# Two head groups in one output bank, three part writes instead of six, and the next x transposed ahead of the maxima

## The chip, the cores and the metric

The kernel runs on one core of one Trainium2 chip. The metric is device time in microseconds from start to end of the whole program. The kernel before took 684.7 us as the median of three runs (683.92 to 686.21).

## What is computed

The input is x, 8 sequences of 512 tokens and 128 features, fp32. It is normalised over its features, and one transformer layer's two halves are added to it side by side:

```python
xn = layernorm(x)
x  = x + attention(xn) + moe(xn)
```

The attention has 16 heads of 8 features, a causal mask, a softmax, and an output projection with a bias. The other half is a mixture of 8 experts (176 hidden columns each, the best 2 per token weighted by a softmax router) and a shared expert of 352 columns; each is `silu(x @ wg) * (x @ wu) @ wd`.

## The kernel before

One sequence of 512 tokens is one block; there are eight. Each engine has its own program, written out by hand in order, and waits on semaphores that count up over the blocks. The steady part is a loop whose pass holds two stages: `attend(i)`, the attention of block i, and `experts_and_maxima(i + 1)`, the expert half of the next block together with the row maxima of its scores. Names and lines below are those of the kernel before.

**Expert stage.** The hidden columns are 14 tiles of 128 (`NT`), in the order `TILE_ORDER`, the three shared ones first. For tile k TensorE computes gate and up (`gate_up`, L457 to L459: an fp32 product out of three reduced ones, six matmuls in all, in the first three of four "ring" banks) and, two tiles later, the down product into `bank_y` (L468 to L470). ScalarE takes the silu (L736) and a rounded copy (L743), GpSimd weighs by the router (L839) and takes the rest of the rounding (L845), VectorE multiplies gate and up (L1066).

**Maxima.** The softmax needs the row maxima ahead. 20 "pairs" of score tiles per block (`scores`, L486, with the mask by L477) are each reduced by VectorE (L1084). `PAIRS_AT[k]` says how many go beside tile k, and `AHEAD = 1` puts pair 0 at the very end of the attention stage before. Pairs 0 to 4 share one pair of banks (the ring's last and `bank_m`), so each waits for the maximum of the one before; from pair `ONE_SLOT` = 5 on, two pairs of banks alternate. Pair 0 waits for `ops_loaded[0]`, pair 10 for `ops_loaded[1]`: the first and second half of the heads' q and k in their split form.

**That split form.** q and k are each written as bf16 parts (`split_q`, `split_k` on VectorE, L981 to L987), sent to DRAM by the SP queue (`q_parts_out`, `k_parts_out`: six DMAs each, three for the heads in the lower half of the partitions and three for the upper), and read back as `q_op` and `k_op` with 6 terms x 8 features = 48 rows a half (`operands_in`, L361 and L363, four DMAs for every half of the heads). SP's order in the loop is: k out, q out, `operands_in` half 0, router weights out and (after they have landed) back in 18 broadcasts (L347), `operands_in` half 1, the store of the output, the maxima out and back (`maxima_in`, L373 and L377).

**End of the expert stage.** When the last pair is reduced, `split_maxima` makes three bf16 parts on VectorE (L1099 to L1106); beside k = 12 TensorE transposes them (`transpose_maxima`, L529), ScalarE copies them out (L753), and SP writes them to DRAM and reads them back as three more rows of `q_op`. VectorE normalises the next block's x (L962) after that split; TensorE transposes it (`transpose_x`, L408) after the maxima, and ScalarE copies it (L710) after the maxima's rows. Then come the next block's k projection and router logits and, when the maxima's rows have landed, the first unit of the attention (L559).

**Attention stage.** It has four groups of four heads, five units a group: TensorE makes transposed scores (`scores_t`, L559), ScalarE the exponentials (L784, 128x1024 each, two such outputs in flight), GpSimd the mask (L872). One group later `weigh_v` (L587) multiplies by v. Every head has 32 output rows, of which 9 are used: 8 features and the row sum from a column of ones in `v_op`. Group g's four heads fill `nat[:, g % 2]`; VectorE copies that bank out (`take_o`, L1113), TensorE transposes it (`transpose_o`, L603) into `o_banks[g]`, VectorE takes reciprocals and multiplies (`normalise_o`, L1119, L1121). So each of these is done four times a block: three of the `transpose_o` stand in the attention stage, one in k = 2 of the next expert stage. The gate and up products of the next block's tiles 0 and 1 stand at the end of the attention stage, between the last parts of `weigh_v`.

Of the kernel before, what the change touches and what calls it, by code (L numbers as in the profile page):

```python
# [13 lines left out]
P = 128  # L14
NB = 8
# [7 lines left out]
GROUPS = H // 4  # L23
NE = 8
# [64 lines left out]
def block_kernel(nc, x, wqkT, wvT, b_qk, b_v, woT, b_o, gateT, w_gu, w_dn, ident, causal, lower, out):  # L89
    ctx = ExitStack()  # L90
    with ctx:
# [41 lines left out]
        v_op = sb("v_op", [P, QT, H, 32])  # L133
# [6 lines left out]
        o_rden = sb("o_rden", [P, QT, 4, 1])  # L140
# [38 lines left out]
        o_banks = [bank_y, bank_m, bank_y, banks[:, 5, :]]  # L179
# [3 lines left out]
        q_dram = nc.dram_tensor("q_dram", [2, TERMS, DH, PAIRS, S], BF16, kind="Internal").ap()  # L183
        k_dram = nc.dram_tensor("k_dram", [2, TERMS, DH, PAIRS, S], BF16, kind="Internal").ap()
# [87 lines left out]
        PART_WRITES = 6  # L272
# [23 lines left out]
        def _(sp):  # L296
            def tokens_in(n):
# [25 lines left out]
            def k_parts_out(j):  # L323
                sp.wait_ge(ksplit_step, 4 * j + 4)
                for s in range(2):
                    own = k_parts[HALF * s:HALF * (s + 1), :, :]
                    for first, n in ((0, 3), (3, 2), (5, 1)):
                        sp.dma_start(k_dram[s, first:first + n].rearrange("t d i n -> (d i) t n"),
                                     own[:, 0:n, :]).then_inc(k_written, 16)

            def q_parts_out(j):
                sp.wait_ge(qsplit_step, 4 * j + 4)
                for s in range(2):
# [15 lines left out]
            def operands_in(j, i, n):  # L349
# [9 lines left out]
                for s in range(2):  # L359
                    rows = slice(HALF * s, HALF * s + SROWS)  # L360
                    sp.dma_start(q_op[rows, own, :], q_dram[s, :, :, own, :].rearrange("t d i n -> (t d) i n")  # L361
                                 ).then_inc(ops_loaded[n], 16)
                    sp.dma_start(k_op[rows, own, :], k_dram[s, :, :, own, :].rearrange("t d i n -> (t d) i n")  # L363
                                 ).then_inc(ops_loaded[n], 16)
# [38 lines left out]
        def _(pe):  # L403
# [57 lines left out]
            def down(b, k, i):  # L461
# [3 lines left out]
                if k == 0 and i is not None:  # L465
                    pe.wait_ge(o_normed, GROUPS * i + 3)
# [22 lines left out]
            def scores(b, i, g, v):  # L489
# [6 lines left out]
                if n == 0:  # L496
                    if i is None:
                        pe.wait_ge(combT_done, 1)
                    else:
                        pe.wait_ge(exp_done, ST_ALL * i + ST_ALL - 1)  # L500
                        pe.wait_ge(o_normed, GROUPS * i + 2)
# [72 lines left out]
            def weigh_v(i, g, c, front):  # L574
# [18 lines left out]
            def transpose_o(i, g, front):  # L593
                pe.wait_ge(o_taken, GROUPS * i + g + 1)
                bank = o_banks[g]
                if g == 0:
                    pe.wait_ge(base_done, i + 1)
                elif g == 1 and front:
                    pe.wait_ge(combT_done, i + 2)
                elif g == 2:  # L600
                    pe.wait_ge(o_normed, GROUPS * i + 1)
                for q in range(QT):
                    mm = pe.transpose(bank[:, q * P:(q + 1) * P], o_sb[:, g % 2, q * P:(q + 1) * P],  # L603
# [3 lines left out]
            def transpose_on(i):  # L607
                pe.wait_ge(o_normed, GROUPS * i + GROUPS)
# [14 lines left out]
            def experts_and_maxima(b, i, front):  # L623

                n = 0 if i is None else AHEAD
                for k in range(NT + 2):
                    if k < NT and (k >= 2 or i is None):
                        gate_up(b, k)
                    if k == 2 and i is not None:
                        transpose_o(i, 3, True)  # L630
                    late = int(k < 4 and PAIRS_AT[k] > 1)
                    for _ in range(PAIRS_AT[k] - late + (AHEAD if k == 0 and i is None else 0)):
# [46 lines left out]
            pe.wait_ge(small_loaded, 13 * 16)  # L679
# [16 lines left out]
            transpose_o(NB - 1, 3, False)  # L696
# [5 lines left out]
        def _(act):  # L702
# [42 lines left out]
            def experts(b, i, front):  # L745
                for k in range(NT):
# [544 lines left out]
```

## Time and profile before

| | |
|---|---|
| profiled execution | 684.85 us, its span 683.1 us |
| median of three runs | 684.7 us |
| TensorE busy | 575.0 us (84%) |
| VectorE / ScalarE / GpSimd busy | 479.9 / 347.6 / 347.7 us |
| mean granted TensorE clock | 0.951 of full |
| moved by DMA | 57.13 MB, 84 GB/s over the span |

The profile is of one execution. Busy time is counted per engine; the span runs from its first instruction to its last. Times in the views are microseconds from the start of the span. One steady block takes 78 to 79 us, and the views below look mostly at one pass, from about 248 us to about 299 us.

### The profile page before, as it was taken

How to read it: one execution, taken by the hardware profiler on the slowest of the kernel's cores; microseconds unless marked ns; L12 is line 12 of the kernel's file. 1: busy time of each engine (PE TensorE's matmuls, PEld its weight loads, DVE VectorE, ACT ScalarE, POOL GpSimd, SP SyncE). 2: the span in 40 equal slices, each digit the busy share in tenths (PEclk: the TensorE clock that was granted, in tenths of full speed). 3: DMA queues.
4: the chain of work that ended last, by engine and by line, in shares of the span. 5: the costliest groups of instructions: out<-in, count | busy, mean ns of one | idle time of the engine just before them, and what ended most of it. 6: DMA issues, size and time to landing. Idle time of an engine off the chain costs nothing.

```text
span 683.1 us, 12744 instructions
## 1 busy us (share of the span) xinstructions
PE 575.0 (84%) x4208; PEld 325.3 (48%) x4208; DVE 479.9 (70%) x829; ACT 347.6 (51%) x472; POOL 347.7 (51%) x330
## 2 busy tenths in 40 slices
PE   1239989799979989899897989899898989799895
PEld 1115652466526653466524653356534654256422
DVE  4947977389656988389665987479774896569713
ACT  1413368233873358533683349533584339543581
POOL 3505735277243854368253764258353773438542
PEclk9759999999999999999999999999999999999987
DMA  6855003830248003750148101660037302480000
GB/s 172 247 123 140 1 22 83 197 64 16 52 93 215 8 13 75 173 107 15 31 102 204 22 21 47 148 161 15 6 92 194 68 15 52 101 209 10 13 2 16
DMA packets 44439, 57.13 MB, mean 84 GB/s; under 512 B 5936, under 2 KB 29840, under 8 KB 44240
## 3 DMA queue, kind: packets, MB, share of 16 engines
q1 hardware_dynamic: 44416, 56.83, 34.4%
q8 instruction: 13, 0.21, 0.1%
q14 instruction: 10, 0.08, 0.0%
HBM read 41.60 MB, written 15.20 MB: 83 GB/s over the span
## 4 chain that ended last, share of the span: by engine, by line
PE 59%; DVE 19%; DMA 9%; issue 6%; SPq 3%; ACT 2%; DVEq 1%; POOLq 0%; POOL 0%; ACTq 0%
PE banks L457 8%; PE banks L459 7%; PE banks L458 7%; PE banks L486 7%; DMA k_op<-k_dram 6%; PE banks L468 5%; PE banks L477 4%; DVE neg_max L1084 4%; PE banks L559 3%; PE banks L587 3%; PE banks L470 3%; PE banks L469 3%; PE banks L603 2%; DVE max_parts L1104 2%; ACT probs L784 1%
## 5 line engine op out<-in xcount | busy, mean ns | idle before, releaser
L1084 DVE TENSOR_REDUCE neg_max<-banks 128x2 f32<-128x1024 f32 (+3 forms) x224 | 194.7, 915 | 71.0 <-PE banks L477 70.1
L784 ACT ACTIVATE probs<-banks 128x1024 f32<-128x1024 f32 x160 | 156.9, 1030 | 19.6 <-PE banks L559 16.5
L839 POOL TENSOR_TENSOR probs<-probs,cb 128x512 f32<-128x512 f32 x88 | 115.9, 1317 | 94.1 <-ACT probs L736 93.2
L845 POOL TENSOR_TENSOR hid_lo<-probs,hid_hi 128x512 fp32r<-128x512 f32 (+1 forms) x88 | 113.4, 1289 | 90.9 <-ACT hid_hi L743 90.9
L736 ACT ACTIVATE probs<-banks 128x512 f32<-128x512 f32 (+1 forms) x112 | 67.0, 598 | 167.9 <-PE banks L459 167.3
L872 POOL TENSOR_SCALAR_AFFINE_SELECT probs<-probs 128x512 f32<-128x512 f32 x128 | 91.9, 739 | 118.9 <-ACT probs L784 118.9
L457 PE MATMUL banks<-x_hi,w_hi 128*128 128x512 f32 (+1 forms) x224 | 96.7, 432 | 2.8 <-DVE w_lo L1230 2.7
L587 PE MATMUL banks<-probs,v_op 128*32 128x512 f32 (+3 forms) x1024 | 95.8, 447 | 0.3
L459 PE MATMUL banks<-x_hi,w_lo 128*128 128x512 f32 (+1 forms) x224 | 92.1, 411 | 0.0
L743 ACT ACTIVATE hid_hi<-probs 128x512 fp32r<-128x512 f32 (+1 forms) x112 | 70.3, 628 | 42.5 <-DVE probs L1066 41.6
L458 PE MATMUL banks<-x_lo,w_hi 128*128 128x512 f32 (+1 forms) x224 | 91.6, 409 | 0.0
L486 PE MATMUL banks<-k_op,q_op 48*128 48x384 bf16 (+3 forms) x512 | 62.0, 304 | 34.5 <-DMA k_op<-k_dram 26.7
L1066 DVE TENSOR_TENSOR probs<-probs,banks 128x512 f32<-128x512 f32 (+1 forms) x112 | 76.0, 680 | 19.8 <-POOL probs L839 10.4
L559 PE MATMUL banks<-q_op,k_op 51*128 51x384 bf16 (+3 forms) x512 | 62.6, 307 | 4.4 <-ACT probs L784 2.3
L468 PE MATMUL banks<-hid_hi,wd_hi 128*128 128x512 f32 (+1 forms) x112 | 56.6, 505 | 2.3 <-DVE hid_lo L1074 2.2
L486 PEld LDWEIGHTS banks<-k_op,q_op 48*128 48x128 bf16 x512 | 19.5, 94 | 75.5 <-issue 34.5
L477 PE MATMUL banks<-mask_half,ident_half 64*128 64x256 bf16 (+1 forms) x640 | 55.3, 250 | 0.0
L559 PEld LDWEIGHTS banks<-q_op,k_op 51*128 51x128 bf16 x512 | 17.6, 94 | 72.9 <-ACT probs L784 42.0
L457 PEld LDWEIGHTS banks<-x_hi,w_hi 128*128 128x128 f32 (+1 forms) x224 | 43.3, 193 | 16.3 <-issue 7.5
L459 PEld LDWEIGHTS banks<-x_hi,w_lo 128*128 128x128 f32 (+1 forms) x224 | 43.8, 196 | 11.2
L458 PEld LDWEIGHTS banks<-x_lo,w_hi 128*128 128x128 f32 (+1 forms) x224 | 44.3, 198 | 8.7
L470 PE MATMUL banks<-hid_lo,wd_hi 128*128 128x512 f32 (+1 forms) x112 | 45.3, 405 | 0.0
(113 smaller groups left out, 634.6 us busy)
## 6 DMA issues: line engine op xcount, KB each, us to landing
cb<-c_dram SPq DMA_DIRECT2D x32, 256.0 KB, 4.3
q_op<-q_dram SPq DMA_DIRECT2D x32, 192.0 KB, 5.6
k_op<-k_dram SPq DMA_DIRECT2D x32, 192.0 KB, 6.2
cb<-c_dram SPq DMA_DIRECT2D x16, 224.0 KB, 4.4
q_dram<-q_parts SPq DMA_DIRECT2D x16, 192.0 KB, 2.7
k_dram<-k_parts SPq DMA_DIRECT2D x16, 192.0 KB, 2.7
cb<-c_dram SPq DMA_DIRECT2D x16, 192.0 KB, 4.5
cb<-c_dram SPq DMA_DIRECT2D x16, 160.0 KB, 4.6
```

Of the source, the lines that this page charges most:

```text
L457: pe.matmul(bank, w_hi[:, w, cols], x_hi[:, :], start=True, stop=False)
L458: pe.matmul(bank, w_hi[:, w, cols], x_lo[:, :], start=False, stop=False)
L459: pe.matmul(bank, w_lo[:, w, cols], x_hi[:, :], start=False, stop=True).then_inc(ready, 1)
L468: pe.matmul(bank_y[:, :], wd_hi[0:n, tile, :], hi, start=(k == 0), stop=False)
L486: pe.matmul(bank[:, a, at:at + n], q_op[own, h // 2, qt * P:n], k_op[own, h // 2, 0:n], start=first, stop=False, skip_group_check=True)
L559: mm = pe.matmul(bank[:, at:at + S - kb * P], k_op[r:r + rows, h // 2, kb * P:(kb + 1) * P], q_op[r:r + rows, h // 2, kb * P:S], start=Tru ...
L587: mm = pe.matmul(nat[32 * j:32 * j + 32, g % 2, kb * P:S], v_op[:, kb, 4 * g + j, :], probs_of(g, j, kb), start=(c == 0), stop=(c == 3), t ...
L784: nc.scalar.activation(probs[:, g % 2, 2 * u:2 * u + 2, :], ring[:, at:at + 2, :], ACT.Exp).then_inc(exp_done, 1)
L839: nc.gpsimd.tensor_tensor(sg[k % 3][:, :], sg[k % 3][:, :], cb[:, TILE_ORDER[k], :], ALU.mult).then_inc(weighted, 1)
L845: nc.gpsimd.tensor_tensor(hid_lo[0:n, k % 3, :], hid[k % 3][0:n, :], hid_hi[0:n, k % 3, :].bitcast(F32), ALU.subtract).then_inc(hid_lo_don ...
L872: return nc.gpsimd.affine_select(out=view, in_=view, compare_op=ALU.is_ge, fill=0.0, base=0, pattern=[[0, 4], [1, P]], channel_multiplier=-1)
L1084: return nc.vector.tensor_reduce(out, in_, AX.X, ALU.max, negate=True)
```

## The change

Three edits.

1. *Output banks.* Groups 0 and 1 accumulate in one bank, groups 2 and 3 in the other. `v_op` gets zeros in the first 9 columns for every odd group, whose own 9 columns come behind them, so that the two groups' sums lie side by side in the 32 rows. `take_o`, `transpose_o` and `normalise_o` then run twice a block, over twice as many columns where they read them. GpSimd places v with four copies instead of one, and `wo_sb` is loaded by four DMAs in the heads' new order instead of one.
2. *Transfers.* The order of the dimensions in the DRAM buffers becomes term, half, feature, pair, token, so each write covers all 128 partitions and there are three a tensor instead of six. The reads keep their number.
3. *Order of work.* Pair 0 moves from the end of the attention stage to k = 1 of the expert stage. The next block's x is normalised on VectorE at tile 0, and transposed and copied before the maxima. The transposed router weights move from (1, 4) to (2, 0) on TensorE, and on VectorE `take_combT` and `split_x` stand before the first `take_o`.

```diff
-AHEAD = 1
-PAIRS_AT = [0 if k < 2 else 2 if k < 11 else int(k == 11) for k in range(NT + 2)]
-ONE_SLOT = AHEAD + 4
+PAIRS_AT = [int(k in (1, 11)) + 2 * int(2 <= k <= 10) for k in range(NT + 2)]
+ONE_SLOT = 5
...
-        v_op = sb("v_op", [P, QT, H, 32])
+        v_op = sb("v_op", [P, QT, 2, H // 2, 32])
...
-        o_banks = [bank_y, bank_m, bank_y, banks[:, 5, :]]
+        o_banks = [bank_y, nat[:, 0, :]]
...
-        q_dram = nc.dram_tensor("q_dram", [2, TERMS, DH, PAIRS, S], BF16, kind="Internal").ap()
+        q_dram = nc.dram_tensor("q_dram", [TERMS, 2, DH, PAIRS, S], BF16, kind="Internal").ap()
...
-                     (wo_sb[:, :], woT), (bo_bc[:, :], b_o.partition_broadcast(P))]
+                     (bo_bc[:, :], b_o.partition_broadcast(P))]
...
+            for j in range(4):
+                sp.dma_start(wo_sb[32 * j:32 * j + 32, :], woT.rearrange("(g j d) e -> j g d e", j=4, d=DH)[j]
+                             ).then_inc(small_loaded, 16)
...
-                for s in range(2):
-                    own = q_parts[HALF * s:HALF * (s + 1), :, :]
-                    for first, n, part in ((0, 3, 0), (3, 2, 1), (5, 1, 2)):
-                        sp.dma_start(q_dram[s, first:first + n].rearrange("t d i n -> (d i) t n"),
-                                     own[:, part:part + 1, :].to_broadcast([HALF, n, S])
-                                     ).then_inc(q_written, 16)
+                for first, n, part in ((0, 3, 0), (3, 2, 1), (5, 1, 2)):
+                    sp.dma_start(q_dram[first:first + n].rearrange("t s d i n -> (s d i) t n"),
+                                 q_parts[:, part:part + 1, :].to_broadcast([P, n, S])).then_inc(q_written, 16)
...
-                    sp.dma_start(q_op[rows, own, :], q_dram[s, :, :, own, :].rearrange("t d i n -> (t d) i n")
-                                 ).then_inc(ops_loaded[n], 16)
+                    sp.dma_start(q_op[rows, own, :], q_dram[:, s, :, own, :]).then_inc(ops_loaded[n], 16)
...
     (weigh_v, TensorE)
-                    if g < 2 and front:
-                        pe.wait_ge((q_done, k_done)[g], i + 2)
-                    if g >= 2:
-                        pe.wait_ge(o_taken, GROUPS * i + g - 1)
+                    if g % 2 == 0 and front:
+                        pe.wait_ge((q_done, k_done)[g // 2], i + 2)
+                bank = nat[:, g // 2, :]
                 for j in range(4):
-                    mm = pe.matmul(nat[32 * j:32 * j + 32, g % 2, kb * P:S], v_op[:, kb, 4 * g + j, :],
-                                   probs_of(g, j, kb), start=(c == 0), stop=(c == 3),
+                    mm = pe.matmul(bank[32 * j:32 * j + 32, kb * P:S], v_op[:, kb, g % 2, 4 * (g // 2) + j, :],
+                                   probs_of(g, j, kb), start=(c == 0 and g % 2 == 0), stop=(c == 3 and g % 2 == 1),
...
     (experts_and_maxima, TensorE, at MAXIMA_AT)
-                        transpose_maxima(b)
                         if front:
                             transpose_x(b + 1)
+                        transpose_maxima(b)
...
     (attend, TensorE)
-                        if u == 2 and g in (2, 3, 4):
-                            transpose_o(i, g - 2, front)
+                        if (g, u) == (3, 2):
+                            transpose_o(i, 0)
                         if front:
-                            if (g, u) == (GROUPS, 1):
-                                pair(i + 1, i, 0)
-                            if (g, u) == (1, 4):
+                            if (g, u) == (2, 0):
                                 transpose_comb(i + 1)
...
     (experts, ScalarE, k == NT - 2)
+                        if front:
+                            take_xT(b + 1)
                         act.wait_ge(mT_ready, b + 1)
...
-                        if front:
-                            take_xT(b + 1)
...
     (experts_and_maxima, VectorE)
+                    if k == 0 and front:
+                        normalise(b + 1)
                     if k == 1 and i is not None:
-                        normalise_o(i, 2)
-                        take_o(i, 3)
+                        take_o(i, 1)
                     if k == 2 and i is not None:
-                        normalise_o(i, 3)
+                        normalise_o(i, 1)
...
     (attend, VectorE, after split_q)
+                    take_combT(i + 1)
+                    split_x(i + 1)
                 take_o(i, 0)
...
```

`k_dram`, `k_parts_out` and the read of `k_op` change as those of q do. The lines in brackets name the place; they are not part of the diff.

## Rows read from the trace of the kernel before

**Rows 1.** The page, busy time by engine: busy us, share of the span, instructions.

```profile
PE 575.0 (84%) x4208; PEld 325.3 (48%) x4208; DVE 479.9 (70%) x829; ACT 347.6 (51%) x472; POOL 347.7 (51%) x330
```

**Rows 2.** The waits of the whole span: total us, times, longest.

```profile
PE banks L486 <- DMA k_op<-k_dram: 26.7, 8, 5.6
```

**Rows 3.** TensorE's timeline, one pass: start, us, line, matmuls, idle before and releaser.

```profile
270.21 0.66 PE L603 MATMUL banks<-ident_sb,o_sb 128*128 128x128 f32 x4 [0.92 <-DVE o_sb L1113]
...
275.43 0.66 PE L603 MATMUL banks<-ident_sb,o_sb 128*128 128x128 f32 x4
...
277.24 1.95 PE L587 MATMUL banks<-probs,v_op 128*32 128x512 f32 x16
281.94 0.61 PE L486 MATMUL banks<-k_op,q_op 48*128 48x512 bf16 x2 [2.75 <-DMA k_op<-k_dram]
...
285.45 0.42 PE L587 MATMUL banks<-probs,v_op 128*32 128x128 f32 x8
...
286.22 0.48 PE L457 MATMUL banks<-x_hi,w_hi 128*128 128x512 f32 x1
...
288.36 0.48 PE L457 MATMUL banks<-x_hi,w_hi 128*96 128x512 f32 x1
...
298.23 0.48 PE L457 MATMUL banks<-x_hi,w_hi 128*128 128x512 f32 x1
...
306.60 0.38 PE L486 MATMUL banks<-k_op,q_op 48*128 48x512 bf16 x2
```

**Rows 4.** ScalarE's timeline of the same pass, the exponentials of the attention.

```profile
260.97 6.69 ACT L784 ACTIVATE probs<-banks 128x1024 f32<-128x1024 f32 x7 [0.25 <-PE banks L559]
...
271.24 4.97 ACT L784 ACTIVATE probs<-banks 128x1024 f32<-128x1024 f32 x5 [1.23 <-PE banks L559]
276.46 1.94 ACT L784 ACTIVATE probs<-banks 128x1024 f32<-128x1024 f32 x2 [0.24 <-PE banks L559]
```

**Rows 5.** TensorE at the end of the expert stage: two rows of that pass, two of the last.

```profile
248.00 0.38 PE L529 MATMUL banks<-ident_bf,max_parts 128*48 128x128 bf16 x4 [1.00 <-DVE max_parts L1106]
...
254.86 0.39 PE L559 MATMUL banks<-q_op,k_op 51*128 51x512 bf16 x2
...
640.73 0.38 PE L529 MATMUL banks<-ident_bf,max_parts 128*48 128x128 bf16 x4 [1.00 <-DVE max_parts L1106]
...
646.06 0.39 PE L559 MATMUL banks<-q_op,k_op 51*128 51x512 bf16 x2 [2.05 <-DMA q_op<-m_dram]
```

**Rows 6.** The SP queue's timeline of the same pass: start, us of issuing, line, DMAs.

```profile
269.58 3.86 SPq L336 DMA_DIRECT2D q_dram<-q_parts  x6
275.28 0.33 SPq L361 DMA_DIRECT2D q_op<-q_dram  x1
...
281.80 8.68 SPq L347 DMA_DIRECT2D cb<-c_dram  x18
290.68 0.30 SPq L361 DMA_DIRECT2D q_op<-q_dram  x1
```

**Rows 7.** Windows: stretch, us, TensorE busy (matmuls), granted clock, DMA share, GB/s.

```profile
276.25:280.50 4.25, 2.91 (x32) 1.00 0.98 186
18.00:21.00 3.00, 3.00 (x8) 1.00 1.02 432
251.25:252.25 1.00, 0.52 (x3) 1.00 0.16 49
125.00:127.00 2.00, 1.82 (x9) 0.50 0.25 83
...
597.00:599.00 2.00, 2.00 (x6) 0.50 0.47 145
```

**Rows 8.** Windows of the second operand read, every engine; then clock, DMA share, GB/s.

```profile
283.00:298.75 15.75, 14.77 (x98) 9.52 (x98) 9.73 (x16) 4.65 (x8) 5.63 (x5) 0.93 0.98 230
```

**Rows 9.** SP's and TensorE's timelines ahead of the loop.

```profile
7.66 0.43 SPq L313 DMA_DIRECT2D wo_sb<-in_woT  x1
...
49.62 0.61 PE L486 MATMUL banks<-k_op,q_op 48*128 48x512 bf16 x2 [5.56 <-DMA k_op<-k_dram]
```

More of the change, by code:

```diff
@@ L23 @@
 GROUPS = H // 4
+OUTS = GROUPS // 2
 NE = 8
@@ L178, in block_kernel @@
         bank_y = banks[:, 7, :]
[L179 removed]
+        o_banks = [bank_y, nat[:, 0, :]]
         nat_pairs = [nat, banks[:, 3:5, :]]
[L183 to L184 removed]
+        q_dram = nc.dram_tensor("q_dram", [TERMS, 2, DH, PAIRS, S], BF16, kind="Internal").ap()
+        k_dram = nc.dram_tensor("k_dram", [TERMS, 2, DH, PAIRS, S], BF16, kind="Internal").ap()
         m_dram = nc.dram_tensor("m_dram", [3, 2, PAIRS, S], BF16, kind="Internal").ap()
@@ L271, in block_kernel @@
         OP_LOADS = 4
-        PART_WRITES = 6
+        PART_WRITES = 3
         XT = NB * QT // 4
@@ L324, in k_parts_out @@
                 sp.wait_ge(ksplit_step, 4 * j + 4)
-                for s in range(2):
[L326 to L329, printed above, removed]
+                for first, n in ((0, 3), (3, 2), (5, 1)):
+                    sp.dma_start(k_dram[first:first + n].rearrange("t s d i n -> (s d i) t n"),
+                                 k_parts[:, 0:n, :]).then_inc(k_written, 16)
             def q_parts_out(j):
                 sp.wait_ge(qsplit_step, 4 * j + 4)
-                for s in range(2):
-                    own = q_parts[HALF * s:HALF * (s + 1), :, :]
-                    for first, n, part in ((0, 3, 0), (3, 2, 1), (5, 1, 2)):
-                        sp.dma_start(q_dram[s, first:first + n].rearrange("t d i n -> (d i) t n"),
-                                     own[:, part:part + 1, :].to_broadcast([HALF, n, S])
-                                     ).then_inc(q_written, 16)
+                for first, n, part in ((0, 3, 0), (3, 2, 1), (5, 1, 2)):
+                    sp.dma_start(q_dram[first:first + n].rearrange("t s d i n -> (s d i) t n"),
+                                 q_parts[:, part:part + 1, :].to_broadcast([P, n, S])).then_inc(q_written, 16)
             def weights_out(j):
@@ L360, in operands_in @@
                     rows = slice(HALF * s, HALF * s + SROWS)
-                    sp.dma_start(q_op[rows, own, :], q_dram[s, :, :, own, :].rearrange("t d i n -> (t d) i n")
-                                 ).then_inc(ops_loaded[n], 16)
-                    sp.dma_start(k_op[rows, own, :], k_dram[s, :, :, own, :].rearrange("t d i n -> (t d) i n")
-                                 ).then_inc(ops_loaded[n], 16)
+                    sp.dma_start(q_op[rows, own, :], q_dram[:, s, :, own, :]).then_inc(ops_loaded[n], 16)
+                    sp.dma_start(k_op[rows, own, :], k_dram[:, s, :, own, :]).then_inc(ops_loaded[n], 16)
             def store(i):
@@ L591, in weigh_v, with transpose_o @@
                     mm.then_inc(pv_done, 1)
[L593 to L596, printed above, removed]
+            def transpose_o(i, a):
+                pe.wait_ge(o_taken, OUTS * i + a + 1)
+                if a == 0:
                     pe.wait_ge(base_done, i + 1)
[L598 to L601, printed above, removed]
                 for q in range(QT):
-                    mm = pe.transpose(bank[:, q * P:(q + 1) * P], o_sb[:, g % 2, q * P:(q + 1) * P],
+                    mm = pe.transpose(o_banks[a][:, q * P:(q + 1) * P], o_sb[:, a, q * P:(q + 1) * P],
                                       ident_sb[:, :])
@@ L629, in experts_and_maxima @@
                     if k == 2 and i is not None:
-                        transpose_o(i, 3, True)
+                        transpose_o(i, 1)
                     late = int(k < 4 and PAIRS_AT[k] > 1)
-                    for _ in range(PAIRS_AT[k] - late + (AHEAD if k == 0 and i is None else 0)):
+                    for _ in range(PAIRS_AT[k] - late):
                         pair(b, i, n)
@@ L825, in _ @@
             nc.gpsimd.memset(k_op[:, :, :], 1.0).then_inc(ones_set, 1)
-            nc.gpsimd.memset(v_op[:, :, :, DH + 1:32], 0.0)
-            nc.gpsimd.memset(v_op[:, :, :, DH:DH + 1], 1.0)
+            for n in range(2):
+                own = (DH + 1) * n
+                if n:
+                    nc.gpsimd.memset(v_op[:, :, n, :, 0:own], 0.0)
+                nc.gpsimd.memset(v_op[:, :, n, :, own + DH + 1:32], 0.0)
+                nc.gpsimd.memset(v_op[:, :, n, :, own + DH:own + DH + 1], 1.0)
             def place_v(j, i):
@@ L833, in place_v @@
                 apart(pool, pool_passed)
-                nc.gpsimd.tensor_copy(v_op[:, :, :, 0:DH], v_new[:, :, :].rearrange(
-                    "p q (h d) -> p q h d", h=H)).then_inc(v_placed, 1)
+                for g in range(GROUPS):
+                    at, own = 4 * (g // 2), (DH + 1) * (g % 2)
+                    last = nc.gpsimd.tensor_copy(
+                        v_op[:, :, g % 2, at:at + 4, own:own + DH],
+                        v_new[:, :, 4 * DH * g:4 * DH * (g + 1)].rearrange("p q (j d) -> p q j d", j=4))
+                last.then_inc(v_placed, 1)
             def weigh_hidden(b, k):
@@ L1163, in experts_and_maxima @@
                         hidden(b, k - 1)
+                    if k == 0 and front:
+                        normalise(b + 1)
                     if k == 1 and i is not None:
-                        normalise_o(i, 2)
-                        take_o(i, 3)
+                        take_o(i, 1)
                     if k == 2 and i is not None:
-                        normalise_o(i, 3)
-                    for _ in range(PAIRS_AT[k] + (AHEAD if k == 0 and i is None else 0)):
+                        normalise_o(i, 1)
+                    for _ in range(PAIRS_AT[k]):
                         pair(b, n)
@@ L1173, in experts_and_maxima @@
                         split_maxima(b)
-                    if n == NAT_ALL and not PAIRS_AT[k] and PAIRS_AT[k - 1] and front:
-                        normalise(b + 1)
                     if k == 6 and i is not None:
@@ L1193, in attend @@
                     split_q(i + 1)
+                    take_combT(i + 1)
+                    split_x(i + 1)
                 take_o(i, 0)
-                if front:
-                    take_combT(i + 1)
                 normalise_o(i, 0)
-                take_o(i, 1)
-                if front:
-                    split_x(i + 1)
-                normalise_o(i, 1)
-                take_o(i, 2)
-                if not front:
-                    normalise_o(i, 2)
-                for n in range(AHEAD if front else 0):
-                    pair(i + 1, n)
             statistics(0)
@@ L1239, in _ @@
             attend(NB - 1, False)
-            take_o(NB - 1, 3)
-            normalise_o(NB - 1, 3)
+            take_o(NB - 1, 1)
+            normalise_o(NB - 1, 1)
             add_attention(NB - 1)
```

41 lines of the change are left out of this document (20 added, 21 removed).

## The prediction

> **What bounds the kernel now.** I read the page first. TensorE is busy 84% of the span and no other engine over 70% [rows 1], so what counts is TensorE's own work and the stretches in which it stands. The waits of the span name one DMA that it stands for: `k_op`, 26.7 us over 8 times [rows 2]. I then read TensorE's timeline over one pass. There it sits idle 2.75 us at pair 0 [rows 3], and the granted clock is 0.50, the lower of its two levels (1.2 GHz), for about 3.4 us after that wait; it falls so in four of the seven passes, the first and the last of which are shown [rows 7]. The other holes are near `take_o` (0.92) and at the end of the expert stage, 1.00 at the maxima [rows 3, 5]. From tile 4 to tile 11 TensorE has no hole, and the change adds and removes nothing there but one wait that I come to.
>
> All terms are for one pass, in the times of the pass shown, and count seven times. They start from the profiled execution, 684.85 us, which stands 0.15 over the median of 684.7.
>
> **End of the expert stage.** Before, 6.86 us go from the maxima's transposes (248.00) to the first unit of the attention (254.86) [rows 5]; in between TensorE waits for the normalised x and transposes it. The change puts both ahead, into the 1.00 us in which TensorE waits for the maxima anyway; four transposes of some 0.6 fit there. What is late next is seen in the last pass, which has no next x: there the unit starts 5.33 after the transposes (646.06 - 640.73) and what releases it is the maxima's read from DRAM. The k projection and the router logits fill the 2.05 of waiting before it nearly whole. So the term is 6.86 - 5.33 = 1.5 saved. It can't be more, as that DMA chain is untouched, and is nothing if ScalarE's copy of x holds up the maxima's rows.
>
> **Attention stage.** Two transposes of o (0.66 each, one of them behind a wait of 0.92) go out of TensorE's way up to the end of `weigh_v` at 279.19, one of the two staying [rows 3]; with the wait that makes 1.6, and two holes behind ScalarE of 0.2 go with them. ScalarE's bound: seven exponentials take 6.69, 0.956 each; sixteen from 260.97 on end at 276.3, where they end at 278.40 now (276.46 + 1.94) [rows 4]. So at most 2.1 can be saved; I take 1.8, `weigh_v` (3, 1) ending at 277.4. The added columns of v cost TensorE nothing, as every head's output had 32 rows already. VectorE loses two copies and two pairs of small operations, which it did while idle: nothing. GpSimd's three more copies and the zeros lie beside its idle time in the shared tiles: nothing; without that cover some 1 us. Normalising beside tile 0 falls on an idle VectorE.
>
> **Pair 0 behind gate and up.** After 277.4 TensorE now has gate and up of tile 0 and `weigh_v` (3, 2), 1.9 at full clock, then tile 1 and `weigh_v` (3, 3), 2.14 (288.36 - 286.22) [rows 3]. It reaches pair 0 at 281.4. The pair takes 0.45, and if the operands are there tile 2 starts at 281.85 instead of 288.36: 6.5 saved. From pair 0 to the first part of `weigh_v` the pass shown took 3.51 (285.45 - 281.94) for what takes 1.85 at full clock, so 1.66 of it is the clock; the three passes of seven without it have that much less to give, 0.7 on average. That leaves 5.8. Between tiles 2 and 4 (9.87 now) one transpose and its wait are replaced by the same in k = 2, and pair 1's maximum follows pair 0's at once; I count 0.2 saved. If operands came in time, a pass would save 1.5 + 5.8 + 0.2 = 7.5.
>
> **The operands.** VectorE's chain to the parts of q isn't shortened, so the writes still start at 269.58. Six issues take 3.86 and the reads start at 275.28, 1.8 behind the last [rows 6]. With three issues the queue is done 1.9 earlier, but the bytes are the same; between nothing and 1.9 I take 0.7 saved, reads issued at 274.6. Data flows from 276.25, 0.95 behind the issue, to 280.50; pair 0 starts 1.4 behind that, 1.2 of it landing [rows 3, 6, 7].
>
> How long does the read's data take? Today 4.25 us at 186 GB/s with the share of the DMA engines at 0.98: 11.6 GB/s for each of 16 [rows 7]. The source of a read was 48 rows evenly apart; with the new layout it is 6 terms of 8 features, its outermost count 6. The trace has one kind of read with so few outer rows, the maxima's three: 49 GB/s at a share of 0.16, that is 2.6 engines busy at 19.1 GB/s each. The weights at the start went at 432 GB/s, 27 for each engine [rows 7]. If the outermost count bounds how many engines carry a transfer, the 790 KB go by six: 4.9 us at 27 each, 6.9 at 19.1, 11.3 at today's 11.6. If it doesn't, 4.25 stays. I take 6.9, the rate of the read nearest in shape, and keep 4.25 and 11.3 as ends.
>
> The Trainium skill (DMA: Bandwidth & Descriptors, "Why a DMA increments its semaphore by 16 and not by 1") says that a transfer uses the largest number of engines up to 16 that divides both sides' slowest dimension: sixteen for the old read, six for the new. No row of this trace numbers the engines, though the maxima's share fits. The page speaks against this change, and what follows where it costs most is the second rival.
>
> With 6.9 the operands are usable at 274.6 + 0.95 + 6.9 + 1.2 = 283.65, so TensorE waits 2.25 for them. Waits of 2.7 to 2.8 brought the clock down in about half the passes; I charge 0.7 for that. SP's queue behind it is the second price. The router weights' write lies behind the reads, the broadcasts start 1.3 after the data (281.80 against 280.50), and the second half's read ends at 298.75, 16.95 after they start, 4.25 of which I put to it [rows 6 to 8]. Now: start at 283.75, data until 283.75 + 12.7 + 6.9 = 303.35, landed 304.55. Pair 10 (306.60, 8.4 after tile 4's start [rows 3]) is now wanted at 281.85 + 2.25 + 0.7 + 9.67 + 8.4 = 302.85. A second wait of 1.7, where before there were some 6 us to spare. The broadcasts themselves are wanted later than they land.
>
> A pass: 7.5 - 2.25 - 0.7 - 1.7 = 2.85 saved, 20 us in seven.
>
> **Ends.** The last attention loses one transpose and its wait: 1 saved. Ahead of the loop `wo_sb` is four issues where one took 0.43 [rows 9]; at 0.64 each, as the writes of three dimensions take [rows 6], about 2 more before TensorE may start (bounds nothing and 3). Pair 0 waits there for its operands too (5.56 [rows 9]), and tile 1's products, 2.6 at the lower clock, move ahead of it into that wait, while the read lasts 2.65 longer and starts 0.7 sooner: 2 - 2.6 + 2.65 - 0.7 = 1.4 lost.
>
> Sum: 684.85 - 20 - 1 + 1.4 = 665 us.
>
> **The rivals.** *The read is quick enough* (chance 0.25). Six engines at 27 GB/s, or sixteen as now. At 4.25 us of data neither wait exists: 7.5 x 7 = 52.5, the end 1, the start 1.3: 630. At 4.9 about 634. For it: the weights' 27 GB/s an engine, and that today's 186 looks like a limit other than the engines', since only 48 partitions are written. Against it: the maxima's 19.1.
>
> *The read takes over the pass* (0.22). Engine for engine no faster than now, 11.3 us of data: wait at pair 0 6.65 and the clock's 1.5, then pair 10 waits 5.3 and again 1.5; 14.95 against 7.5 saved, 52 lost in seven passes, and 5.8 at the start less 1: 742. At 9.6 us, two engines at a time sharing what one could have: 716. It decides from 8.0 us of data on (16.4 GB/s an engine), where waits and clock eat the 7.5. For it: the share of 0.98 at 186 GB/s. Against it: six engines ask for less at once from whatever limits sixteen.
>
> *The tail gives nothing* (0.1). ScalarE reaches the copy of x late and the maxima's rows go out later, or the first unit waits longer for their read: 1.5 x 7 off, 675. Against it: ScalarE is only 51% busy over the span [rows 1] and has nothing between the last silu and the maxima's rows.
>
> **Chances.** The forecast, 665, has 0.40, with its own range 645 to 688 for reads of 5.5 to 8 us; 0.03 is left for what I don't see. Measurement of this kernel tells 0.3% (2 us) from no change. From the cases: faster 0.74, same 0.04, slower 0.22. The range that holds 8 in 10 takes in the quick read and the milder half of the slow one: 629 to 716.
>
> **What would show it.** Right: no idle at L408, the first L559 of the attention released by the maxima's read, 5.3 behind L529; pair 0 behind tile 1 with a wait of about 2 for `k_op`; a DMA share near 0.4 while the reads run, over 6.9 us; pair 10 waiting for `k_op`. If the share stays near 1 over 4.3 us, the first rival holds. If the data last over 8 us and both pairs wait long at the lower clock, the second does. Wrong in another way: `weigh_v` (3, 1) ending no earlier against the stage's first unit, or GpSimd's copies of v delaying the router's weighting at tile 3.

## The result and the profile after

The changed kernel takes 645.3 us, median of 4 runs (641.3 to 646.8); the kernel before, run beside it, 685.5 (683.9 to 688.2). The ratio is 0.940 (95% interval 0.934 to 0.946), so some 40 us are saved where 20 were forecast. The profiled run took 641.28 us with a span of 639.6, against 684.85 and 683.1 before.

The page of the changed kernel, busy time by engine; it answers to [rows 1]:

```profile
PE 556.5 (87%) x4144; PEld 312.1 (49%) x4144; DVE 462.7 (72%) x781; ACT 347.4 (54%) x472; POOL 343.3 (54%) x357
```

TensorE lost 18.5 us of work and some 25 of standing. The waits of the span (total, times, longest), which answer to [rows 2]:

```profile
PE banks L482 <- DMA k_op<-k_dram: 11.3, 6, 6.5
```

6.5 of that is ahead of the loop. Within the seven passes the wait fell from 21.1 us (26.7 less 5.6) to 4.8.

The granted clock is 1.00 through all seven passes of this profile. Before, it fell once in each of the seven and cost 1.7 us each time, 12 in all: in four passes behind the wait at pair 0, and in the other three behind the wait for the next x at the end of the expert stage, which the prediction doesn't name. Such a wait in the kernel before:

```profile
171.65 0.65 PE L408 MATMUL banks<-ident_sb,xn 128*128 128x128 f32 x4 [1.35 <-DVE xn L962]
```

and windows behind this wait and behind that of the next pass, where the clock stayed:

```profile
172.00:177.00 5.00, 5.00 (x18) 0.66 0.04 12
250.00:255.00 5.00, 4.46 (x25) 1.00 0.05 15
```

From the maxima's transposes to the first unit the three passes took 7.7 to 7.8 us, the other four 6.7 to 6.9.

TensorE's timeline of the changed kernel in the pass shown before, then the same instruction in the last pass, then ahead of the loop; it answers to [rows 3, 5, 9]:

```profile
236.72 0.38 PE L525 MATMUL banks<-ident_bf,max_parts 128*48 128x128 bf16 x4 [0.59 <-DVE max_parts L1102]
...
242.07 0.39 PE L555 MATMUL banks<-q_op,k_op 51*128 51x512 bf16 x2 [0.41 <-DMA q_op<-m_dram]
...
263.24 1.95 PE L582 MATMUL banks<-probs,v_op 128*32 128x512 f32 x16
265.12 0.50 PE L453 MATMUL banks<-x_hi,w_hi 128*128 128x512 f32 x1
...
268.66 0.64 PE L582 MATMUL banks<-probs,v_op 128*32 128x256 f32 x8
269.24 0.39 PE L482 MATMUL banks<-k_op,q_op 48*128 48x512 bf16 x2
...
597.75 0.38 PE L525 MATMUL banks<-ident_bf,max_parts 128*48 128x128 bf16 x4 [1.03 <-DVE max_parts L1102]
...
52.06 0.61 PE L482 MATMUL banks<-k_op,q_op 48*128 48x512 bf16 x2 [6.55 <-DMA k_op<-k_dram]
```

The first of the seven passes begins with these transposes at 91.16, so a pass takes (597.75 - 91.16) / 7 = 72.37; before it took (640.73 - 89.68) / 7 = 78.72. That is 6.35 a pass and 44.5 in seven; 1.5 is lost ahead of the loop and 0.5 won in the last attention: the 43.5 between the spans.

Pair 0, at 269.24, waits for nothing here. It does in two of the seven passes (124.98 and 341.69), and pair 10 in three (the third waits 0.18):

```profile
124.98 0.39 PE L482 MATMUL banks<-k_op,q_op 48*128 48x512 bf16 x2 [1.34 <-DMA k_op<-k_dram]
...
216.56 0.39 PE L482 MATMUL banks<-k_op,q_op 48*128 48x512 bf16 x2 [0.68 <-DMA k_op<-k_dram]
...
341.69 0.39 PE L482 MATMUL banks<-k_op,q_op 48*128 48x512 bf16 x2 [0.73 <-DMA k_op<-k_dram]
...
577.60 0.39 PE L482 MATMUL banks<-k_op,q_op 48*128 48x512 bf16 x2 [1.78 <-DMA k_op<-k_dram]
```

The SP queue's timeline of the changed kernel (start, us of issuing), which answers to [rows 6]:

```profile
256.66 1.44 SPq L335 DMA_DIRECT2D q_dram<-q_parts  x3
260.30 0.76 SPq L359 DMA_DIRECT2D q_op<-q_dram  x1
...
268.87 8.72 SPq L345 DMA_DIRECT2D cb<-c_dram  x18
277.79 0.78 SPq L359 DMA_DIRECT2D q_op<-q_dram  x1
```

Windows of the changed kernel (stretch, us, TensorE busy, granted clock, DMA share, GB/s): the writes, the first half's read, the second half's:

```profile
257.50:259.75 2.25, 1.79 (x20) 1.00 1.00 350
262.50:267.50 5.00, 4.97 (x44) 1.00 0.39 144
282.00:286.80 4.80, 4.80 (x37) 1.00 0.37 146
```

The reads start 3.64 us after the writes, where it was 5.70 [rows 6]. Their data moves at a share of 0.39 and 144 GB/s, where 0.98 and 186 stood [rows 7], so it flows longer, from about 261.5 to 267.9.

### The profile page after: what moved, and what is told of

Read it like the earlier page. It is cut to its first block, busy times and chain, and to the rows that moved or that the text cites. A ratio compares the mean times of both kernels' runs of the same rounds, so it can differ in the third digit from the quotient of the medians.

```text
span 639.6 us, 12491 instructions
## 1 busy us (share of the span) xinstructions
PE 556.5 (87%) x4144; PEld 312.1 (49%) x4144; DVE 462.7 (72%) x781; ACT 347.4 (54%) x472; POOL 343.3 (54%) x357
## 4 chain that ended last, share of the span: by engine, by line
PE 46%; DMA 17%; DVE 13%; SPq 11%; issue 6%; ACT 5%; POOL 1%; POOLq 0%; DVEq 0%; ACTq 0%
SPq L345 5%; PE banks L482 5%; DMA k_op<-k_dram 5%; PE banks L453 5%; PE banks L582 5%; PE banks L455 5%; PE banks L454 5%; PE banks L464 4%; ACT probs L772 4%; PE banks L555 4%; PE banks L473 3%; DMA c_dram<-combT 3%; DMA q_op<-m_dram 3%; DVE neg_max L1080 3%; PE banks L465 2%
## 5 line engine op out<-in xcount | busy, mean ns | idle before, releaser
L772 ACT ACTIVATE probs<-banks 128x1024 f32<-128x1024 f32 x160 | 155.0, 1034 | 15.8 <-PE banks L555 13.5
L868 POOL TENSOR_SCALAR_AFFINE_SELECT probs<-probs 128x512 f32<-128x512 f32 x128 | 85.3, 688 | 116.3 <-ACT probs L772 116.3
L1062 DVE TENSOR_TENSOR probs<-probs,banks 128x512 f32<-128x512 f32 (+1 forms) x112 | 75.5, 680 | 33.5 <-PE banks L455 15.1
L453 PE MATMUL banks<-x_hi,w_hi 128*128 128x512 f32 (+1 forms) x224 | 94.1, 420 | 4.5 <-DVE w_lo L1215 2.7
L455 PE MATMUL banks<-x_hi,w_lo 128*128 128x512 f32 (+1 forms) x224 | 89.7, 400 | 0.0
L454 PE MATMUL banks<-x_lo,w_hi 128*128 128x512 f32 (+1 forms) x224 | 89.2, 398 | 0.0
L455 PEld LDWEIGHTS banks<-x_hi,w_lo 128*128 128x128 f32 (+1 forms) x224 | 42.2, 188 | 10.7
L454 PEld LDWEIGHTS banks<-x_lo,w_hi 128*128 128x128 f32 (+1 forms) x224 | 42.4, 189 | 8.1
L465 PE MATMUL banks<-hid_hi,wd_lo 128*128 128x512 f32 (+1 forms) x112 | 44.8, 400 | 0.0
```

The costliest lines, as they stand in the source:

```text
L453: pe.matmul(bank, w_hi[:, w, cols], x_hi[:, :], start=True, stop=False)
L454: pe.matmul(bank, w_hi[:, w, cols], x_lo[:, :], start=False, stop=False)
L455: pe.matmul(bank, w_lo[:, w, cols], x_hi[:, :], start=False, stop=True).then_inc(ready, 1)
L772: nc.scalar.activation(probs[:, g % 2, 2 * u:2 * u + 2, :], ring[:, at:at + 2, :], ACT.Exp).then_inc(exp_done, 1)
L868: return nc.gpsimd.affine_select(out=view, in_=view, compare_op=ALU.is_ge, fill=0.0, base=0, pattern=[[0, 4], [1, P]], channel_multiplier=-1)
```

## The experiments

Theory A: the gain is pair 0's move behind gate and up, which lets the operands' chain run beside TensorE's work; the new transfers are themselves a loss. Its rivals: the quicker writes and their new layout bring the gain (B), or the edits are each worth their own forecast wherever they stand. "Changed" is the kernel after the change. The pass length is worked out as above, from each kernel's profiled run.

### The old transfers in the changed kernel (undo_transfers)

```diff
-        q_dram = nc.dram_tensor("q_dram", [TERMS, 2, DH, PAIRS, S], ...
+        q_dram = nc.dram_tensor("q_dram", [2, TERMS, DH, PAIRS, S], ...
-        PART_WRITES = 3
+        PART_WRITES = 6
     (six writes of 64 partitions and reads of (t d) rows, as before)
```

> The changed kernel with the old DRAM layout: six writes a tensor, reads with 48 outermost rows. Theory A (the two halves of edit 2 cancel): parts land about 2.0 us later as before the change, the operand read takes 4.3 us of data instead of 6.0 to 6.6, so pair 0 finds its operands within 0.3 us of where it does now, and the waits at pair 10 go: within 0.5% of the changed kernel, 642 to 648 us. Rival B (the earlier writes carry part of the gain): each pass loses 1.5 to 2 us at pair 0: 655 to 660. Rival C (the read on fewer engines costs most of what the writes bring, as I had forecast it): faster than the changed kernel by over 1%, under 638.

633.5 us (632.8 to 635.4), ratio to the kernel before 0.928 (0.923 to 0.932), pass 71.82: quicker than the changed kernel. I had expected the two halves of edit 2 to cancel (642 to 648); what came is rival C of the text above, faster than the changed kernel by over 1%. Of all kernels here that compute the reference it has the lowest time, with rows_by_feature (below) within the intervals. The old transfers are better by 0.012 of the time, some 8 us. SP's queue, TensorE and a window of the read in this kernel:

```profile
250.96 3.83 SPq L339 DMA_DIRECT2D q_dram<-q_parts  x6
256.67 0.32 SPq L364 DMA_DIRECT2D q_op<-q_dram  x1
```

```profile
259.41 0.50 PE L460 MATMUL banks<-x_hi,w_hi 128*128 128x512 f32 x1
...
263.53 0.39 PE L489 MATMUL banks<-k_op,q_op 48*128 48x512 bf16 x2
```

```profile
257.60:261.60 4.00, 3.97 (x31) 1.00 1.00 200
```

From the first write's issue to the end of the read's data it takes 10.6 us (to 261.6), in the changed kernel 11.2 (256.66 to 267.9). What the writes won the reads gave back, and more. Both reach pair 0 4.1 us behind tile 0's first product; here nothing waits for `k_op` in the seven passes but one pair for 0.96. B falls. Of the 8.6 us between the two profiled spans (639.6 and 631.0), 4.3 lie ahead of the loop (first transposes of the maxima at 91.16 and 86.89), where the wait for `k_op` is 6.55 against 2.75, and 3.9 in the seven passes, where it is 4.8 against 1.0.

### Three writes, and reads of 48 rows (read_48_rows)

```diff
-  sp.dma_start(q_op[rows, own, :], q_dram[:, s, :, own, :]) ...
+  sp.dma_start(q_op[rows, own, :], q_dram.rearrange("t s d i n -> (t s d) i n")[48 * s:48 * s + 48, own, :]) ...
```

It reads as many bytes, but the wrong rows of the buffer, so the scores are not the reference's.

> The changed kernel with its three writes, but the operand reads take 48 consecutive rows of the DRAM buffer each (the wrong rows, so the attention's values are not the reference's; bytes, DMAs and waits are the same). Theory A: the outermost count decides how many engines carry the read: DMA share near 1.0 instead of 0.39, data in about 4.3 us instead of 6.0 to 6.6, issue 0.4 us a DMA instead of 0.7; the waits for k_op (0.7 us a pass, 6.5 ahead of the loop) all but go: 5 to 8 us faster than the changed kernel, about 638. Rival: the DMA share stays near 0.4, then the number of rows isn't what decides, and the time is the changed kernel's.

632.9 us (630.6 to 633.5), ratio 0.925 (0.920 to 0.930), pass 71.59, no wait for `k_op` in the loop. The read in the same pass:

```profile
257.10:261.10 4.00, 3.97 (x45) 1.00 0.98 201
```

With the three writes kept and only the shape of the reads changed, the whole loss goes, about 10 us, more than the 5 to 8 that I expected. So the reads are the price of edit 2, and the quicker writes buy no more than the difference to undo_transfers, which is within the intervals.

### Feature outermost (rows_by_feature)

```diff
-  sp.dma_start(q_op[rows, own, :], q_dram[:, s, :, own, :]) ...
+  sp.dma_start(q_op[rows, own, :], q_dram[:, s, :, own, :].rearrange("t d i n -> d t i n")) ...
```

The rows of both operands come in the order feature, term; the scores stay what they were.

> The changed kernel with the 48 operand rows in the order feature, term instead of term, feature (q and k alike, so the result is the reference's); the read's outermost count is then 8, not 6. Theory A (the outermost count is the number of engines): DMA share 0.50 instead of 0.39 while the read runs, data in 4.5 to 5.2 us instead of 6.0 to 6.6 unless the partitions written limit it, pair 10 no longer waits: 3 to 6 us faster than the changed kernel. Rival: share and length of the read stay, time unchanged.

634.5 us (633.5 to 636.9), ratio 0.929 (0.926 to 0.931), pass 71.70, no wait for `k_op` in the loop.

```profile
257.50:261.50 4.00, 3.96 (x35) 1.00 0.48 164
```

Eight outer rows instead of six: the share goes from 0.39 to 0.48, the data takes some 5.2 us instead of 6.4, and nearly all of the loss is gone. That is more than I expected; a read that ends 1.2 us sooner is already in time for both pairs.

### The changed kernel again (changed_again)

> The changed kernel once more, beside the others of this call, to measure what its six-engine read costs against the kernel with the old transfers (0.9277 of the time before). Theory A: the transfers of the change cost about 1%: 0.937 to 0.944 of the time before here too. Rival: the gap to the old transfers was a matter of the chip or the call: 0.927 to 0.932.

643.6 us (639.4 to 647.8), ratio 0.940 (0.937 to 0.943). In its profile the seven passes take 71.6 to 76.7 us. The longest has another DMA late, the maxima's, with the clock at its lower level after the wait:

```profile
312.38 0.33 SPq L369 DMA_DIRECT2D m_dram<-max_rows  x1
315.50 0.56 SPq L373 DMA_DIRECT2D q_op<-m_dram  x2
```

```profile
318.27 0.61 PE L555 MATMUL banks<-q_op,k_op 51*128 51x512 bf16 x2 [1.99 <-DMA q_op<-m_dram]
```

That write took 3.1 us from issue to the read's, where 1.6 is usual. Why it does now and then isn't known; it is part of the wider spread of this kernel's times. The second longest, 75.5, waits for `k_op` at pair 0 (0.74) and at pair 10, and behind the second wait the clock falls:

```profile
217.82 0.39 PE L482 MATMUL banks<-k_op,q_op 48*128 48x512 bf16 x2 [1.48 <-DMA k_op<-k_dram]
```

```profile
218.00:223.00 5.00, 5.00 (x30) 0.66 0.00 0
```

So the slow read can cost the clock too, 1.7 us here, though it didn't in the first profile.

### Pair 0 back at the end of the attention (undo_pair0)

```diff
-PAIRS_AT = [int(k in (1, 11)) + 2 * int(2 <= k <= 10) for k in range(NT + 2)]
+AHEAD = 1
+PAIRS_AT = [0 if k < 2 else 2 if k < 11 else int(k == 11) for k in range(NT + 2)]
...
+                            if (g, u) == (GROUPS, 1):
+                                pair(i + 1, i, 0)
```

> The changed kernel with pair 0 back at the end of the attention stage, before tile 0's gate and up. Theory A: TensorE reaches it 265.1 against operands at about 268.8, waits 3.5 us and more a pass, and the granted clock falls to 0.50 after it in half the passes or more: 4.0 to 5.0 us a pass against 0.3 now, 27 to 33 us slower, 672 to 678. Rival B (the operands come early enough since the writes are quicker): wait under 2 us, no fall of the clock, 8 to 14 us slower, about 656.

683.2 us (680.1 to 688.1), ratio 1.001 (0.998 to 1.004): without this one edit the change is worth nothing. That is some 42 us, more than the 27 to 33 that I expected. The waits, pair 0 in the pass shown, and TensorE's windows around pair 0 in three of the seven passes:

```profile
PE banks L483 <- DMA k_op<-k_dram: 37.4, 8, 8.5
```

```profile
282.66 0.61 PE L483 MATMUL banks<-k_op,q_op 48*128 48x512 bf16 x2 [4.07 <-DMA k_op<-k_dram]
```

```profile
281.00:290.00 9.00, 7.34 (x35) 0.62 0.61 181
...
439.00:448.00 9.00, 6.24 (x35) 0.81 0.54 167
596.00:605.00 9.00, 8.62 (x51) 0.81 0.76 199
```

The same windows of the kernel before, three of the seven:

```profile
202.00:211.00 9.00, 6.32 (x44) 1.00 0.61 166
281.00:290.00 9.00, 8.06 (x46) 0.81 0.73 196
...
518.00:527.00 9.00, 8.28 (x57) 1.00 0.78 206
```

The waits in the loop grow from 21.1 to 28.9 us, since everything ahead of pair 0 became shorter and the operands' chain did not. The clock's share grows too. A mean of 0.81 over 9 us is about 1.7 us lost (9 x 0.19), one of 0.62 about 3.4. Around pair 0 four passes had the first before and three nothing; here four have the second and three the first. Over the whole of the seven passes, the falls elsewhere included, the lower level cost 12 us before and 22 here, a little of it while TensorE stood anyway. So some 8 + 10 = 18 us go, most of the 23 that x ahead and the output banks bring when pair 0 doesn't wait (15 + 8, below).

### x ahead of the maxima taken back (undo_x_ahead)

```diff
+                        transpose_maxima(b)
                         if front:
                             transpose_x(b + 1)
-                        transpose_maxima(b)
     (ScalarE's copy of x and VectorE's normalise likewise)
```

> The changed kernel with x normalised after the split of the maxima, and transposed and copied after them, as before. Theory A: each of the seven passes gets back the 1.5 us between the maxima's transposes and the first unit of the attention (5.35 to 6.86): 10.5 us slower, about 655. Rival: the freed end is bound by the maxima's read anyway and ScalarE's order doesn't matter: under 3 us slower.

653.7 us (652.8 to 654.5), ratio 0.956 (0.951 to 0.960), pass 74.12. TensorE in that pass:

```profile
240.08 0.38 PE L525 MATMUL banks<-ident_bf,max_parts 128*48 128x128 bf16 x4 [1.03 <-DVE max_parts L1102]
241.81 1.11 PE L404 MATMUL banks<-ident_sb,xn 128*128 128x128 f32 x4 [1.35 <-DVE xn L958]
...
247.56 0.39 PE L555 MATMUL banks<-q_op,k_op 51*128 51x512 bf16 x2
```

The wait for x is back, and 7.48 us lie between the maxima and the first unit where the changed kernel has 5.35. That is more than the 6.86 of the pass shown before, as the clock falls behind this wait here; it does so in four of the seven passes.

### Single edits on the kernel before

Each takes its lines of the diff alone: banks_only edit 1 together with the moves of the router weights' transposes, `take_combT` and `split_x` out of edit 3, so that "output banks" below means all of these; before_pair0 the move of pair 0 alone; before_x_ahead the normalising and transposing of x alone; before_pair0_x both of the last two.

> The output banks alone (with the moves of the router weights' transposes, take_combT and split_x that come with them); pair 0, the transfers and x as in the kernel before. Theory A: TensorE's shorter attention stage only brings it sooner to pair 0, whose operands hang on VectorE's chain and SP, so that of 1.2 us a pass most turns into a longer wait there (about 4 us instead of 2.9) and a lower clock more often; only the transposes of o behind pair 0 count: 3 to 7 us faster than before, 0.990 to 0.996. Rival: the shorter stage counts whole, 12 us or more: under 0.983.

683.6 us (680.8 to 685.5), ratio 1.001 (0.999 to 1.002), pass 78.48: nothing, where I expected 3 to 7 us. The waits for `k_op` say where it went, 32.6 us over 8 times instead of 26.7, of which 5.7 more in the loop; the lower level costs 13.7 us in the seven passes instead of 12:

```profile
PE banks L490 <- DMA k_op<-k_dram: 32.6, 8, 5.8
```

> The kernel before with one thing changed: pair 0 at k = 1 of the expert stage, behind gate and up of tiles 0 and 1. Theory A: its operands come 2.5 us after TensorE wanted them before and gate and up take 2.9 at full clock, so the wait of 2.7 to 2.9 a pass and the low clock after it (1.66 in four of seven) go: 3.6 to 4.0 us a pass, 25 to 30 us faster, 652 to 660. Rival (pair 0's maximum and those of pairs 1 and 2 now queue on VectorE in k = 1 and 2, and TensorE waits for them): half of it, 668 or more.

656.4 us (654.7 to 657.1), ratio 0.961 (0.958 to 0.964), pass 74.78, as expected. The wait is gone with nothing in the transfers changed:

```profile
263.96 0.33 SPq L360 DMA_DIRECT2D q_op<-q_dram  x1
```

```profile
272.32 0.39 PE L485 MATMUL banks<-k_op,q_op 48*128 48x512 bf16 x2
```

> The kernel before with x alone ahead: normalised at tile 0, transposed and copied before the maxima. Theory A: the end of the expert stage gives its 1.5 us a pass whole, since VectorE's chain to the parts of q starts with the attention stage and comes sooner as well: 10 us faster, 0.984 to 0.987. Rival (like the output banks, it only moves TensorE sooner to a wait): no change.

673.4 us (671.0 to 679.5), ratio 0.988 (0.982 to 0.994), pass 77.01: 8 us, with the 0.984 to 0.987 expected inside the interval and no change outside it. The pass lengths give 12 (1.71 x 7); the single runs go from 671.0, the profiled one, to 679.5.

> The kernel before with pair 0 behind tile 1 and x ahead; output banks and transfers as before. Theory A: the output banks, worth nothing by themselves (1.0005), are worth their 1.2 to 1.7 us a pass once pair 0 no longer waits; so this kernel lies 9 to 13 us over the one with the old transfers and all else changed (0.9277): 0.942 to 0.947 of the time before. Rival (the banks are worth nothing here either): 0.928 to 0.932.

642.0 us (641.2 to 642.9), ratio 0.939 (0.936 to 0.943), pass 72.94. Against undo_transfers (0.928), which is this plus the output banks, they are worth 0.012, some 8 us, once pair 0 doesn't wait, a little less than the 9 to 13 expected. The two ran on different chips, each against its own runs of before; the difference of the ratios is known to about 0.006.

The whole, in us at 683 (ratio differences; pass lengths in brackets, us a pass):

```
pair 0 behind gate and up, alone       27 saved  (78.72 -> 74.78)
  taken out of the whole change        42 lost   (72.37 -> 78.32)
x ahead, alone                          8 saved  (78.72 -> 77.01)
  on top of pair 0                     15 saved  (74.78 -> 72.94)
  taken out of the whole change        11 lost   (72.37 -> 74.12)
output banks, alone                     0        (78.72 -> 78.48)
  on top of pair 0 and x                8 saved  (72.94 -> 71.82)
transfers, on top of all that           8 lost   (71.82 -> 72.37)
```

## Why the prediction was right and wrong

The direction, the place of the gain and its order were right; the amount was half of what came. Step by step:

- *End of the expert stage*, 1.5 a pass: the mechanism was right. The first unit comes 5.35 behind the maxima's transposes (242.07 - 236.72), forecast 5.33, and what releases it is the maxima's read. The size was a little low: the pass lengths give 1.7 to 1.8. The 6.86 came from a pass at full clock; in three of seven the stretch took 7.7 or more, 7.2 on average, since the clock fell behind the wait for x. "It can't be more" left that out.
- *Attention stage*, 1.8: too high. From the first unit to the end of `weigh_v` (3, 1) it took 24.33 before (254.86 to 279.19) and takes 23.1 now, 1.2 saved; before_pair0_x against undo_transfers gives 1.1.
- *Pair 0 behind gate and up*: right. It is reached 4.1 behind `weigh_v` (3, 1), forecast 4.0. The move was to bring 5.8 - 1.8 + 0.2 = 4.2 a pass and alone gave 3.94. From another side: the seven waits of before, 21.1 / 7 = 3.0, and 0.7 of the clock, which lost 12 us in the loop before and 6.8 in before_pair0, make 3.7. The clock no longer falls behind pair 0 there, but it falls behind the wait for x in four passes instead of three.
- *The sum without waits*, 7.5: 6.35 plus the 0.68 of waits measured is 7.0. By the pass lengths of the single edits the attention stage lacks 0.7 of what I gave it and pair 0 0.3, and the end of the expert stage gave 0.3 more.
- *The operands*: here it failed. I forecast 4.65 a pass (2.25 at pair 0, 0.7 of the clock, 1.7 at pair 10) and 0.68 was measured: 0.30 at pair 0, 0.38 at pair 10, and the granted clock is 1.00 behind each of the four waits shown above. The mechanism was there (a share of 0.39 while the reads run, waits at both pairs in some passes); the sizes were wrong. Four did it. (a) The writes were bounded by "the bytes are the same", 0 to 1.9 sooner; the reads went out 2.06 sooner, outside my bounds, because the bytes themselves moved faster, 350 GB/s where the row of before (it stands with the last section) has 197. (b) The read's data took 6.4 us, not 6.9: six engines at 24 GB/s each. (c) Those two, 1.4 and 0.5, with a stage that ends 0.6 later than forecast, turn a wait of 2.25 into one of about nothing, and without the wait there is nothing for the clock to take. (d) At pair 10 I put the read's added 2.65 behind the broadcasts' time; from the first broadcast's issue to the end of the read's data took 17.9 (268.87 to 286.8), not 19.6: the read begins while the broadcasts still flow, and from 278 to 281 both together have a share of 1.00 to 1.09.
- *Ends*: 1.4 and 1 forecast, 1.5 lost and 0.5 saved measured. That `wo_sb`'s four issues would hold the start up was wrong: the first transposes of x came at 12.71, before at 13.03. The longer wait there, 6.55 instead of 5.56, made up for it. So the number 1.4 is luck: the operands were to come 3.95 later and came 2.4 later (52.06 against 49.62), and tile 1's products moved ahead of them saved 1.0, not 2.6.

So the term that failed is the operands': waits and clock were to take 4.65 of the 7.5 that the order of work frees; they took 0.68. Of the rivals, the quick read came nearest. Its time, 630 to 634, is near that of the three kernels whose reads are quick (632.9, 633.5, 634.5). The read took over no pass: 6.4 us of data is well short of its 8.0.

On how many engines carry the read: six outer rows gave a share of 0.39 (6/16 is 0.375), eight 0.48 (0.50), forty-eight 0.98. The Trainium skill's rule (DMA: Bandwidth & Descriptors, "Why a DMA increments its semaphore by 16 and not by 1"), the largest number up to 16 that divides the slowest dimension of both sides, gives six, eight and sixteen; the shares agree, though no view numbers the engines. What the prediction took from it, that the new read would be the slower, was right, and is worth some 8 us.

Open: the split of those 8 us, 3.9 in the loop and 4.3 ahead of it, is that of two single profiles, and the two profiles of the changed kernel differ by nearly as much (spans 639.6 and 646.0, passes 72.37 and 73.32). Also not shown is why the clock fell after some waits of about 2.8 us and not after others.

## What to carry to other kernels

Before shortening what precedes a wait, find the chain that the waiting instruction depends on: with that chain fixed, a shorter stage only lengthens the wait, and the clock takes more on top (the output banks were worth nothing, and 8 us once pair 0 no longer waited). Move independent work in front of the wait first; the other edits are paid from then on. When a DMA's layout is changed, read both sides: three writes that cover all partitions were quicker, and the reads that they made necessary lost it again; the same rows in an order with an outermost count of 8 got nearly all of it back.

## What the runs showed of the hardware

*Writes that left from 128 partitions moved faster than writes from 64.* With the same bytes, six writes from 64 partitions moved at 197 GB/s and three from 128 at 350 (above). Issuing doesn't explain it: the six carry 3, 2 and 1 terms for 0.64 us of issuing each, and yet in quarters of a microsecond, but for the first and the last, their rate stays between 176 and 221 GB/s. The number of the writes and the layout in DRAM changed along with the partitions, and no run separates the three. The window of before:

```profile
270.75:274.75 4.00, 3.77 (x39) 1.00 0.82 197
```

The issues went from 0.64 us each to 0.48.

*Six engines carry over two thirds of what sixteen carry into 48 partitions.* 144 GB/s with six, 164 with eight, 186 to 201 with sixteen, so with the engine counts read from the shares one moves 24, 21 and 12 GB/s. The sixteen are busy at half the rate that the six reach, so something other than an engine's own rate bounds them; the runs don't show what. A read of 6 x 8 rows costs 0.7 us of SP's queue to issue, one of 48 rows 0.3 to 0.4.

*After long waits the clock fell every time, after shorter ones only sometimes.* In the loops of before, banks_only and undo_pair0 there are fifteen waits for `k_op` of 3.3 us and more, and the clock went to its lower level with every one: ten times 1.7 us were lost, five times, with waits of 4.1 to 5.5, 3.4, of which some fell into the wait itself. After the thirteen waits of 2.2 to 3.0 us of before and before_x_ahead seven times 1.7 were lost; it happened after one of 2.20 and not after one of 3.01. Among waits of 1.35 (for x, before) three of six were followed by it. So the length of the wait doesn't decide alone.
